# One-core transformer block with expert routing: the expert weights are transposed by VectorE in 32x32 blocks and SBUF transfers in place of TensorE, and the engines' orders are rewritten

## Chip, core, metric

The kernel runs on one core of a Trainium2 chip. The metric is the device time of one execution in microseconds (us), taken as the median over several executions. Everything is computed in fp32.

## What is computed

The input is 8 sequences of 2048 tokens with 256 features. Cut to what matters, the reference is:

```python
x = x + layernorm(attention(layernorm(x)))        # causal linear attention in chunks of 128 tokens, plus a memory part
x = x + layernorm(ffn(layernorm(x)))

def ffn(h):                                       # 4 heads, 64 keys a side, 1024 experts, 8 taken per head
    sx, ix = top_k(h @ Wq[x] @ keys[x], 8); sy, iy = top_k(h @ Wq[y] @ keys[y], 8)
    scores, indices = top_k(sx[:, None] + sy[None, :], 8)
    w = silu((h . down_embed[indices]) * softmax(scores))
    return silu(h @ W_up.T) @ W_down.T + sum(w * up_embed[indices])
```

## The kernel before

The tokens are cut into 128 tiles of 128 tokens, each tile one chunk of one sequence, sequences in turn. Nothing is gathered: for each tile and head a full row of 1024 expert weights per token is built (`wexp[:, h, :]`, 128 x 1024), which is zero outside the chosen experts. The four rows are added into `wexp[:, 3, :]`, that sum is transposed to `gT` (experts on partitions), and `y` gets the product of `gT` with the centred `up_embed` (`ue`).

The work of a tile is spread over `STAGES` = 8 steps. The helper `pipeline(body)` calls `body` once a step on each engine, with `t[k]` the tile that is in stage k at this step (the tile that entered k steps ago). Each engine has its own `body`, and the statements in it are that engine's order in a step, written out by hand. Waits on named semaphores tie the engines together.

- TensorE (PE): its products go through `product` (L511), its transposes of normed activations through `turn` (L516). In a step it multiplies with `route`, `wvo`, `wdownT`, `deT`, `state`, `mem_x`, `ue`, `wupT`, `wqT` and `wkT`. For tile `t[5]` it transposes `wexp[:, 3, :]` in eight 128x128 pieces into two PSUM banks (L587, L591), after a wait on `heads_summed`.
- ScalarE (ACT): moves PSUM to SBUF and computes Exp, Silu and Square. It copies the two transposed banks to `gT` (L692, L703). A step loads four activation tables (Silu and Exp alternate).
- VectorE (DVE): selection by threshold (`picked`) and multiplication with the softmax (`prob`), four each of 128x1024 a step (L768, L784, L843, L851; L776, L780, L788, L861), maxima, layernorm statistics.
- GpSimd (POOL): `key_sums` (L401, four of 128x1024 a step), the powers for layernorm (L387), small tensors, and it issues two accumulating transfers inside SBUF: L441 adds heads 0 and 2 to 1 and 3 (1024 KB, `head_pairs_summed`), L409 adds head 1 to 3 (512 KB, `heads_summed`).
- SyncE (SP) issues the store of `x_out` (L355) and the load of `x_in` (L360), one each a step.

The `gT` product for tile `t[6]` waits for both copies of a step before:

```python
pe.wait_ge(s_expert_weights_T_0_ready, t[6] + 1)
pe.wait_ge(s_expert_weights_T_1_ready, t[6] + 1)
product(y_ps, EC, lambda c: gT[:, t[6] % 2, c, :], lambda c: ue[:, c, :], start=False)
```

Of the kernel before, what the change touches and what calls it, by code (L numbers as in the profile page):

```python
# [6 lines left out]
def sandwich_kernel(nc, hidden, w_q, w_k, w_v, w_o, gate, memory, memory_norm,  # L7
# [33 lines left out]
    HALF = 512  # L41
    LAST_IN = EXPERTS - 1
# [8 lines left out]
    SLOTS = 4  # L51
# [11 lines left out]
    with ctx:  # L63
# [26 lines left out]
        x_mid = sb("x_mid", [P, SLOTS, D])  # L90
# [34 lines left out]
        z_last = sb("z_last", [P, NC])  # L125
        w_last = sb("w_last", [P, 2])
# [6 lines left out]
        gT = sb("gT", [P, 2, EC, P])  # L133
# [33 lines left out]
        g_ps = (bank[5], bank[3])  # L167
# [29 lines left out]
        s_mem_in_psum = sem("mem_in_psum")  # L197
        s_num_in_psum = sem("num_in_psum")
# [42 lines left out]
        s_expert_weights_T_0_in_psum = sem("expert_weights_T_0_in_psum")  # L241
        s_expert_weights_T_1_in_psum = sem("expert_weights_T_1_in_psum")
        s_expert_weights_T_0_ready = sem("expert_weights_T_0_ready")
        s_expert_weights_T_1_ready = sem("expert_weights_T_1_ready")
# [4 lines left out]
        s_x_stored = sem("x_stored")  # L249
        s_head_0_sums_ready = sem("head_0_sums_ready")  # L250
# [27 lines left out]

        def alone(eng):

            eng.sem_inc(s_passed, 1)

        STAGES = 8

        def pipeline(body):


            for step in range(TILES + STAGES - 1):
                body([t if 0 <= t < TILES else None for t in range(step, step - STAGES, -1)],
                     STAGES + SLOTS <= step < TILES)  # L290

# [3 lines left out]
        def chunk_of(t):  # L295
            return t // BATCH

        KEPT = TILES - BATCH
# [39 lines left out]
        def _(sp):  # L338
# [13 lines left out]
            def body(t, steady):  # L352
                if t[7] is not None:
                    sp.wait_ge(s_x_out_ready, t[7] + 1)
                    sp.dma_start(out_tiles[:, chunk_of(t[7]), seq_of(t[7]), :], x_out[:, :]).then_inc(s_x_stored, 16)  # L355
                if t[0] is not None:
                    wait(sp, s_x_loaded, 16 * t[0])
                    if not steady:
                        wait(sp, s_x_mid_ready, t[0] - 3)
                    sp.dma_start(x_in[:, t[0] % SLOTS, :], x_tiles[:, chunk_of(t[0]), seq_of(t[0]), :]).then_inc(s_x_loaded, 16)  # L360

# [4 lines left out]
        def _(pool):  # L366
# [39 lines left out]
            def body(t, steady):  # L406
                if t[6] is not None:
                    pool.wait_ge(s_head_pairs_summed, 16 * (t[6] + 1))
                    pool.dma_start(wexp[:, HEADS - 1, :], wexp[:, 1, :], accum_op=ALU.add).then_inc(s_heads_summed, 16)  # L409
                if t[5] is not None:  # L410
                    pool.wait_ge(s_cand_exp_ready, t[5] + 1)
                    pool.wait_ge(s_cand_mask_ready, t[5] + 1)
                    nc.gpsimd.tensor_tensor(cprob[:, :, :], cmask[:, :, :], cdif[:, :, 0:NCAND], ALU.mult).then_inc(s_cand_prob_ready, 1)  # L413
                if t[4] is not None:
                    pool.wait_ge(s_x_mid_var_eps, t[4] + 1)
                    power(LN_M, t[4] % 2).then_inc(s_x_mid_rstd, 1)
                if t[5] is not None:
                    pool.wait_ge(s_softmax_inverses, t[5] + 1)
                    pool.wait_ge(s_cand_prob_ready, t[5] + 1)
                    nc.gpsimd.tensor_tensor(z_last[:, :].rearrange("p (h n) -> p h n", h=HEADS), cprob[:, :, :],  # L420
                                            per_head(rz[:, t[5] % 2, :], NCAND), ALU.mult).then_inc(s_last_expert_in_ready, 1)
                    pool.wait_ge(s_head_0_weights_ready, t[5] + 1)
                    pool.wait_ge(s_last_expert_weight, t[5] + 1)
                    nc.gpsimd.tensor_tensor(wexp[:, 0, LAST_IN:], wexp[:, 0, LAST_IN:], w_last[:, t[5] % 2:t[5] % 2 + 1], ALU.add).then_inc(s_last_expert_added, 1)  # L424
                if t[7] is not None:
                    pool.wait_ge(s_y_var_eps, t[7] + 1)
                    power(LN_Y, t[7] % 2).then_inc(s_y_rstd, 1)
# [8 lines left out]
                if t[5] is not None:  # L436
                    pool.wait_ge(s_head_1_weights_ready, t[5] + 1)
                    pool.wait_ge(s_head_2_weights_ready, t[5] + 1)
                    pool.wait_ge(s_head_3_weights_ready, t[5] + 1)
                    pool.wait_ge(s_last_expert_added, t[5] + 1)  # L440
                    pool.dma_start(wexp[:, 1::2, :], wexp[:, 0::2, :], accum_op=ALU.add).then_inc(s_head_pairs_summed, 16)  # L441
                if t[4] is not None:
# [4 lines left out]
                    nc.gpsimd.tensor_tensor(neg_max[:, t[4] % 2, :], zero[:, :], best[:, :, 0], ALU.subtract).then_inc(s_neg_max_ready, 1)  # L447
                    key_sums(2).then_inc(s_head_2_sums_ready, 1)
                    key_sums(3).then_inc(s_head_3_sums_ready, 1)
                if t[1] is not None:  # L450
                    pool.wait_ge(s_x_var_eps, t[1] + 1)
                    power(LN_X, t[1] % 2).then_inc(s_x_rstd, 1)
                if t[3] is not None:
                    pool.wait_ge(s_mix_var_eps, t[3] + 1)
                    power(LN_O, t[3] % 2).then_inc(s_mix_rstd, 1)
# [4 lines left out]
        def _(pe):  # L460
# [60 lines left out]
            def body(t, steady):  # L521
# [367 lines left out]
```

## Time and profile before

| | |
|---|---|
| three runs | 3052.66, 3050.07, 3050.55 us; median 3050.55 us |
| profiled execution | 3049.49 us, with a span of 3047.8 us |
| busy, of the span | TensorE 98%, its weight loads 80%, ScalarE 86%, VectorE 71%, GpSimd 60% |
| mean granted TensorE clock | 0.995 of full speed |
| transfers | 244.17 MB, mean 80 GB/s |

The time of an execution is the span plus what lies around it, here 1.7 us. An engine is busy while one of its instructions runs; for TensorE matmuls overlap in the records, so a matmul's own duration is longer than the distance to the next one. The profile names an operation by its line in the kernel, its output and its inputs. An fp32 matmul stands in the trace as two records, a transpose by TensorE as one. A duration is followed in square brackets by the idle time ahead of it and by the work that ended this idle time.

### The profile page before, as it was taken

The numbers are of one execution on the slowest core, as the hardware profiler recorded it, in microseconds if no ns is written. First come the engines' busy times: TensorE is split into PE (matmuls) and PEld (weight loads), VectorE is DVE, ScalarE is ACT, GpSimd is POOL, SyncE is SP. The second block draws the span as 40 slices with busy tenths as digits, with TensorE's granted clock in tenths as the row PEclk, the third lists the DMA queues.
The fourth block names the chain that finished last, engine by engine and source line by source line (L and its number), as shares of the span: only waits on it lengthen the run. The fifth ranks groups of instructions, "written<-read, shape, count | busy, mean of one in ns | idle before, by whom it ended". The sixth has DMA issues, their size and how long they took to land.

```text
span 3047.8 us, 48454 instructions
## 1 busy us (share of the span) xinstructions
PE 3001.7 (98%) x16426; PEld 2446.1 (80%) x16426; DVE 2169.6 (71%) x5636; ACT 2622.7 (86%) x4106; POOL 1821.7 (60%) x2455
## 2 busy tenths in 40 slices
PE   6999999999999999999999999999999999999997
PEld 5788888888888888888888888888888888888886
DVE  4777777767776777777677767776777777677774
ACT  4988888888888888888888888888888888888985
POOL 2665665566566656655665666566556655665664
PEclk8999999999999999999999999999999999999999
DMA  3443444344334434443444344334434443443443
GB/s 92 81 85 73 81 83 80 77 82 83 75 77 86 81 74 79 85 80 75 81 83 78 77 84 83 74 77 87 81 73 80 83 80 77 81 83 76 82 85 71
DMA packets 96202, 244.17 MB, mean 80 GB/s; under 512 B 8659, under 2 KB 46548, under 8 KB 95956
## 3 DMA queue, kind: packets, MB, share of 16 engines
q0 software_dynamic: 53248, 201.34, 36.7%
q1 hardware_dynamic: 42708, 39.73, 4.4%
q8 instruction: 132, 2.16, 0.3%
q14 instruction: 114, 0.93, 0.1%
HBM read 22.94 MB, written 16.78 MB: 13 GB/s over the span
## 4 chain that ended last, share of the span: by engine, by line
PE 96%; DMA 1%; issue 1%; ACT 0%; POOL 0%; DVE 0%; SPq 0%; POOLq 0%; DVEq 0%
PE banks L511 84%; PE banks L563 3%; PE banks L516 2%; PE banks L547 2%; PE banks L587 2%; PE banks L591 2%; PE banks L550 1%; DMA wexp<-wexp 1%; DMA sums<-in_L_ffn_keys_dram 0%; SPq L345 0%; POOL sums L401 0%; PE banks L502 0%; PE banks L495 0%; PE banks L480 0%; DVE prob L861 0%
## 5 line engine op out<-in xcount | busy, mean ns | idle before, releaser
L401 POOL TENSOR_TENSOR sums<-scores 128x1024 f32<-128x1024 f32 x512 | 1076.6, 2218 | 392.8 <-ACT scores L636 392.8
L511 PEld LDWEIGHTS banks<-xn2T,wupT 128*128 128x128 f32 x4096 | 477.3, 192 | 9.2 <-DVE state L848 2.7
L511 PE MATMUL banks<-deT,xn2T 128*128 128x512 f32 x1024 | 481.3, 592 | 0.0
L511 PE MATMUL banks<-xn2T,wupT 128*128 128x128 f32 x4096 | 478.2, 275 | 1.9 <-DVE state L848 1.9
L511 PE MATMUL banks<-wdownT,hT 128*128 128x256 f32 x2048 | 464.4, 380 | 0.0
L511 PE MATMUL banks<-ue,gT 128*128 128x256 f32 x2048 | 462.9, 379 | 0.0
L511 PEld LDWEIGHTS banks<-wdownT,hT 128*128 128x128 f32 x2048 | 390.1, 191 | 53.7 <-issue 0.5
L511 PEld LDWEIGHTS banks<-ue,gT 128*128 128x128 f32 x2048 | 388.6, 190 | 53.8 <-issue 0.7
L387 POOL TENSOR_TENSOR rstd<-var_eps,minus_half 128x1 f32<-128x1 f32 x512 | 329.9, 704 | 56.3 <-DVE var_eps L829 38.2
L413 POOL TENSOR_TENSOR cprob<-cmask,cdif 128x112 f32<-128x112 f32 x128 | 65.9, 515 | 396.6 <-DVE cmask L751 396.6
L511 PEld LDWEIGHTS banks<-deT,xn2T 128*128 128x128 f32 x1024 | 185.3, 190 | 129.9 <-issue 122.9
L424 POOL TENSOR_TENSOR wexp<-wexp,w_last 128x1 f32<-128x1 f32 x128 | 26.2, 205 | 364.7 <-ACT z_last L696 364.7
L511 PE MATMUL banks<-route,xn2T 128*128 128x512 f32 x512 | 242.2, 596 | 0.7 <-ACT xn2T L700 0.7
L804 DVE SCALAR_TENSOR_TENSOR sig<-banks,rqk 128x512 f32<-128x512 f32 x128 | 88.5, 691 | 193.9 <-ACT banks L642 193.9
L843 DVE SCALAR_TENSOR_TENSOR picked<-sums,cand_best,banks 128x1024 f32<-128x1024 f32 x128 | 163.9, 1280 | 62.0 <-PE banks L511 62.0
L654 ACT COPY sk_nat<-banks 128x256 f32<-128x256 f32 x120 | 44.6, 372 | 176.1 <-PE banks L550 176.1
L820 DVE TENSOR_SCALAR dens<-banks 128x2 f32<-128x2 f32 x128 | 20.5, 160 | 246.6 <-PE banks L547 246.6
L788 DVE SCALAR_TENSOR_TENSOR prob<-picked,rz,prob 128x1024 f32<-128x1024 f32 x128 | 164.5, 1285 | 13.7 <-DVE picked L784 0.5
L682 ACT ACT_TABLE_LOAD x128 | 164.2, 1283 | 2.3
L650 ACT ACT_TABLE_LOAD x127 | 162.9, 1283 | 2.2
L861 DVE SCALAR_TENSOR_TENSOR prob<-picked,rz,prob 128x1024 f32<-128x1024 f32 x128 | 164.3, 1284 | 0.0
L776 DVE SCALAR_TENSOR_TENSOR prob<-picked,rz,prob 128x1024 f32<-128x1024 f32 x128 | 163.9, 1281 | 0.0
(140 smaller groups left out, 7244.3 us busy)
## 6 DMA issues: line engine op xcount, KB each, us to landing
wexp<-wexp POOLq DMA_DIRECT2D x128, 1024.0 KB, 7.9
wexp<-wexp POOLq DMA_DIRECT2D x128, 512.0 KB, 4.7
x_in<-_attn_hidden_states_dram SPq DMA_DIRECT2D x128, 128.0 KB, 2.1
out_dram<-x_out SPq DMA_DIRECT2D x128, 128.0 KB, 1.7
wexp<-in_L_ffn_W_up_dram SPq DMA_DIRECT2D x1, 1024.0 KB, 7.1
prob<-in_L_ffn_down_embed_dram SPq DMA_DIRECT2D x1, 1024.0 KB, 9.6
ue<-in_L_ffn_up_embed_dram SPq DMA_DIRECT2D x1, 1024.0 KB, 12.0
wexp<-in_L_ffn_W_down_dram SPq DMA_DIRECT2D x1, 1024.0 KB, 13.0
```

Source lines behind the costliest of these rows:

```text
L387: return nc.gpsimd.tensor_tensor(rstd[:, n, m:m + 1], var_eps[:, n, m:m + 1], minus_half[:, :], ALU.pow)
L401: return nc.gpsimd.tensor_tensor(sums[:, k, :, :], scores[:, k, 0:XIN].unsqueeze(2).broadcast_to([P, XIN, NKEYS]), scores[:, HEADS + k, :] ...
L413: nc.gpsimd.tensor_tensor(cprob[:, :, :], cmask[:, :, :], cdif[:, :, 0:NCAND], ALU.mult).then_inc(s_cand_prob_ready, 1)
L511: last = nc.tensor.matmul(out, lhs(c), rhs(c), start=(start and c == 0), stop=(stop and c == chunks - 1))
L563: last = nc.tensor.matmul(ds_ps[:, c, :], sk_nat[:, c * P:(c + 1) * P], v_one[:, :], start=True, stop=True)
L650: nc.scalar.activation(cdif[:, :, :], cdif[:, :, :], ACT.Exp).then_inc(s_cand_exp_ready, 1)
L682: nc.scalar.activation(flat(hT[:, t[4] % 2, 4:8, :]), u_ps[1][:, :], ACT.Silu).then_inc(s_hidden_1_ready, 1)
L776: nc.vector.scalar_tensor_tensor(prob[:, 1, :], picked[:, 1, :], rz[:, t[5] % 2, 1:2], prob[:, 1, :], ALU.mult, ALU.mult).then_inc(s_head_ ...
L788: nc.vector.scalar_tensor_tensor(prob[:, 3, :], picked[:, 1, :], rz[:, t[5] % 2, 3:4], prob[:, 3, :], ALU.mult, ALU.mult).then_inc(s_head_ ...
L804: nc.vector.scalar_tensor_tensor(sig[:, t[3] % 2, :, :], eqk, 1.0, rqk[:, :, :], ALU.min, ALU.add).then_inc(s_sigma_ready, 1)
L843: nc.vector.scalar_tensor_tensor(picked[:, 0, :], head(sums, 0), best[:, 0, TOP - 1:TOP], down, ALU.is_ge, ALU.mult).then_inc(s_head_0_sel ...
L861: nc.vector.scalar_tensor_tensor(prob[:, 0, :], picked[:, 0, :], rz[:, t[4] % 2, 0:1], prob[:, 0, :], ALU.mult, ALU.mult).then_inc(s_head_ ...
```

## The change

- The eight PE transposes and the two ACT copies are gone, and with them four semaphores. DVE now transposes all 32x32 blocks of `wexp[:, 3, :]` in one instruction into a new SBUF tensor `w_blocks`; it waits for `heads_summed` and for the moves of the tile before.
- SP then moves the blocks between groups of 32 partitions: sixteen transfers a step, each of 32 rows of 1 KB.
- `gT` is laid out `[P, 2, P, EC]` (token, then chunk), so that a row of a moved block is contiguous. The stationary operand of the `ue` product is `gT[:, s, :, c]`, whose 128 elements in a partition are 8 elements (32 bytes) apart.
- The pipeline has 10 stages in place of 8, `x_in` has 8 slots in place of 4, and `x_mid` has 8.
- The order of all engines in a step is rewritten, and several operations belong to another stage than before.

```diff
-    SLOTS = 4
+    SLOTS = 8
+    MID_SLOTS = 8
...
+        w_blocks = sb("w_blocks", [P, EXPERTS])
...
-        gT = sb("gT", [P, 2, EC, P])
+        gT = sb("gT", [P, 2, P, EC])
...
+        def moved(eng, sems, t, dmas, most=TILES):
+
+            if 0 <= t < most:
+                eng.wait_ge(sems[t % 2], 16 * dmas * (t // 2 + 1))
...
-        STAGES = 8
+        STAGES = 10
...
+                if t[7] is not None:
+                    sp.wait_ge(s_expert_weights_blocks_turned, t[7] + 1)
+                    for i in range(BLOCKS):
+                        for j in range(BLOCKS):
+                            sp.dma_start(gT[j * BLOCK:(j + 1) * BLOCK, t[7] % 2, i * BLOCK:(i + 1) * BLOCK, :],
+                                         w_blocks[i * BLOCK:(i + 1) * BLOCK, j * BLOCK * EC:(j + 1) * BLOCK * EC]
+                                         .rearrange("p (t c) -> p t c", c=EC)).then_inc(s_expert_weights_blocks_moved[t[7] % 2], 16)
...
-                if t[5] is not None:
-                    pe.wait_ge(s_heads_summed, 16 * (t[5] + 1))
-                    for k in range(4):
-                        e = k
-                        last = nc.tensor.transpose(g_ps[0][:, k * P:(k + 1) * P], wexp[:, HEADS - 1, e * P:(e + 1) * P], ident[:, :])
-                    last.then_inc(s_expert_weights_T_0_in_psum, 1)
...
+                if t[3] is not None:
+                    pe.wait_ge(s_xn1T_ready, t[3] + 1)
+                    product(v_ps, DC, lambda c: xn1T[:, c, :], lambda c: wvo[:, c, :]).then_inc(s_v_in_psum, 1)
+                    wait(pe, s_hidden_1_ready, t[3] - 1)
...
+                if t[7] is not None:
+                    moved(pe, s_expert_weights_blocks_moved, t[7], BLOCKS ** 2)
+                    product(y_ps, EC, lambda c: gT[:, t[7] % 2, :, c], lambda c: ue[:, c, :], start=False).then_inc(s_y_in_psum, 1)
...
+                    wait(act, s_expert_weights_blocks_turned, t[6])
+                    nc.scalar.activation(wexp[:, 3, :], prob[:, 3, :], ACT.Silu).then_inc(s_head_3_weights_ready, 1)
...
-                    act.wait_ge(s_expert_weights_T_0_in_psum, t[5] + 1)
-                    nc.scalar.copy(flat(gT[:, t[5] % 2, 0:4, :]), g_ps[0][:, :]).then_inc(s_expert_weights_T_0_ready, 1)
...
+            def blocks(x):
+                return x.rearrange("p (c j q) -> p j c q", j=BLOCKS, q=BLOCK)
+
+            def turned_blocks(x, chunks):
+                return x[:, :].rearrange("p (j t c) -> p j c t", j=BLOCKS, c=chunks)
+
...
+                    dve.wait_ge(s_heads_summed, 16 * (t[7] + 1))
+                    moved(dve, s_expert_weights_blocks_moved, t[7] - 1, BLOCKS ** 2)
+                    nc.vector.transpose(turned_blocks(w_blocks, EC), blocks(wexp[:, HEADS - 1, :])).then_inc(s_expert_weights_blocks_turned, 1)
```

TensorE before, from the product with `ue` to the next step's first products (`wupT` gives the hidden layer, `ident` marks a transpose):

```order
L511 MATMUL banks<-ue,gT 128x256 [waits expert_weights_T_1_ready,expert_weights_T_0_ready]
L511 MATMUL banks<-ue,gT 128x256 x7
L511 MATMUL banks<-xn2T,wupT 128x128 [waits state_ready]
L511 MATMUL banks<-xn2T,wupT 128x128 x15
L587 MATMUL banks<-ident,wexp 128x128 [waits heads_summed]
L587 MATMUL banks<-ident,wexp 128x128 x3
L591 MATMUL banks<-ident,wexp 128x128 x4
L516 MATMUL banks<-ident,xn 128x128 [waits xn2_ready,xn1T_ready]
L516 MATMUL banks<-ident,xn 128x128
L511 MATMUL banks<-xn1T,wqT 128x128 [waits hidden_1_ready,xn1T_ready]
```

And in the changed kernel, from the first half of the `wupT` products to the transpose of `xn2`, behind which `state` and `route` follow:

```order
L523 MATMUL banks<-xn2T,wupT 128x128 [waits state_ready]
L523 MATMUL banks<-xn2T,wupT 128x128 x7
L523 MATMUL banks<-wvo,xn1T 128x256 [waits xn1T_ready]
L523 MATMUL banks<-wvo,xn1T 128x256
L523 MATMUL banks<-xn1T,wqT 128x128 [waits hidden_1_ready]
L523 MATMUL banks<-xn1T,wqT 128x128 x3
L523 MATMUL banks<-xn1T,wkT 128x128 x4
L523 MATMUL banks<-xn2T,wupT 128x128 x8
L523 MATMUL banks<-ue,gT 128x256 [waits expert_weights_blocks_moved_1]
L523 MATMUL banks<-ue,gT 128x256 x7
L528 MATMUL banks<-ident,xn 128x128 [waits xn2_ready]
```

The transposes are gone, the `wupT` products stand in two halves with `wvo` and the `wqT`, `wkT` products between them, and the wait on `hidden_1_ready` (the Silu of the first half, which frees its PSUM bank) stands two `wvo` matmuls behind that half.

GpSimd in the changed kernel, from the candidate differences of a tile (behind its first two key sums) to the power that the next `xn2` waits for (`cmask` of DVE is waited for as cand_mask_ready):

```order
L466 TENSOR_TENSOR cdif<-cand_best 128x144 [waits best_ready]
L421 TENSOR_TENSOR wexp<-wexp,w_last 128x1 [waits head_0_weights_ready,last_expert_weight]
L423 TENSOR_TENSOR neg_max<-zero,cand_best 128x4
L429 DMA wexp<-wexp 128x2x1024 [waits head_1_weights_ready,head_3_weights_ready,head_2_weights_ready,last_expert_added]
L412 TENSOR_TENSOR sums<-scores 128x1024
L398 TENSOR_TENSOR rstd<-var_eps,minus_half 128x1 [waits mix_var_eps]
L438 TENSOR_TENSOR cprob<-cmask,cdif 128x112 [waits cand_mask_ready,cand_exp_ready]
L412 TENSOR_TENSOR sums<-scores 128x1024
L442 TENSOR_TENSOR z_last<-cprob,rz 128x112 [waits softmax_inverses,cand_prob_ready]
L446 DMA wexp<-wexp 128x1024 [waits head_pairs_summed]
L398 TENSOR_TENSOR rstd<-var_eps,minus_half 128x1 [waits x_var_eps]
L398 TENSOR_TENSOR rstd<-var_eps,minus_half 128x1 [waits x_mid_var_eps]
```

The power for `xn2` (waits x_mid_var_eps) now stands behind the issue of the second accumulating transfer, which waits for the first to land.

SyncE in the changed kernel, a step and the start of the next:

```order
L361 DMA x_in<-in_L_attn_hidden_states_dram 128x256 [waits x_loaded]
L364 DMA out_dram<-x_out 128x256 [waits x_out_ready]
L369 DMA gT<-w_blocks 32x256 [waits expert_weights_blocks_turned]
L369 DMA gT<-w_blocks 32x256 x15
L361 DMA x_in<-in_L_attn_hidden_states_dram 128x256 [waits x_loaded]
```

The sixteen moves are new on this queue; the load of `x_in` stands ahead of the store.

## Rows read from the trace of the kernel before

**Rows 1.** First part of the page: busy time of each engine.

```profile
PE 3001.7 (98%) x16426; PEld 2446.1 (80%) x16426; DVE 2169.6 (71%) x5636; ACT 2622.7 (86%) x4106; POOL 1821.7 (60%) x2455
```

**Rows 2.** Busy time by stretch: PE, PEld, DVE, ACT, POOL, granted clock, DMA share, GB/s.

```profile
190.00:1400.00 1210.00, 1210.00 (x6649) 987.11 (x6648) 876.81 (x2280) 1062.24 (x1664) 735.95 (x988) 1.00 0.42 80
```

**Rows 3.** Waits of TensorE for others: us in total, times, longest us.

```profile
PE banks L587 <- DMA wexp<-wexp: 13.4, 3, 10.5
```

**Rows 4.** Chain that ended last, one step: start us, us, what.

```profile
1535.82 11.73 PE banks L511 x56
...
1558.04 0.44 PE banks L587 x4
1558.47 0.44 PE banks L591 x4
...
1559.13 11.73 PE banks L511 x56
```

**Rows 5.** Timeline of TensorE, same step: start us, us, engine, line, operation.

```profile
1539.16 1.03 PE L511 MATMUL banks<-wvo,xn1T 128*128 128x256 f32 x4
1540.03 3.62 PE L511 MATMUL banks<-wdownT,hT 128*128 128x256 f32 x16
...
1550.85 3.62 PE L511 MATMUL banks<-ue,gT 128*128 128x256 f32 x16
1554.30 3.73 PE L511 MATMUL banks<-xn2T,wupT 128*128 128x128 f32 x32
```

**Rows 6.** Groups by line: busy us, mean ns of one, idle before.

```profile
L682 ACT ACTIVATE hT<-banks 128x512 f32<-128x512 f32 x128 | 76.4, 597 | 1.4
L703 ACT COPY gT<-banks 128x512 f32<-128x512 f32 x128 | 76.1, 595 | 0.3 <-PE banks L591 0.3
L387 POOL TENSOR_TENSOR rstd<-var_eps,minus_half 128x1 f32<-128x1 f32 x512 | 329.9, 704 | 56.3 <-DVE var_eps L829 38.2 <-ACT y_sq L688 14.4 <-DVE var_eps L763 2.1
L861 DVE SCALAR_TENSOR_TENSOR prob<-picked,rz,prob 128x1024 f32<-128x1024 f32 x128 | 164.3, 1284 | 0.0
L729 DVE SCALAR_TENSOR_TENSOR ue<-row_sum,ue 128x2048 f32<-128x2048 f32 x1 | 2.3, 2291 | 0.0
```

**Rows 7.** Timeline near the end: ScalarE hands over to the waiting TensorE.

```profile
2995.71 0.36 ACT L700 COPY xn2T<-banks 128x256 f32<-128x256 f32 x1
2996.12 0.30 PEld L511 LDWEIGHTS banks<-route,xn2T 128*128 128x128 f32 x2 [0.90 <-ACT xn2T L700]
```

**Rows 8.** Timeline of the SP queue, at the start and in the step of rows 4.

```profile
1.95 0.47 SPq L345 DMA_DIRECT2D sums<-in_L_attn_memory_dram  x1
2.45 0.46 SPq L345 DMA_DIRECT2D sums<-in_L_attn_w_q_dram  x1
...
1539.63 0.43 SPq L360 DMA_DIRECT2D x_in<-_attn_hidden_states_dram  x1
```

**Rows 9.** DMA issues: KB each, median us from issue to landing.

```profile
wexp<-wexp POOLq DMA_DIRECT2D x128, 1024.0 KB, 7.9
wexp<-wexp POOLq DMA_DIRECT2D x128, 512.0 KB, 4.7
x_in<-_attn_hidden_states_dram SPq DMA_DIRECT2D x128, 128.0 KB, 2.1
...
sums<-in_L_attn_w_q_dram SPq DMA_DIRECT2D x1, 256.0 KB, 3.7
```

**Rows 10.** Timeline of GpSimd in the same step.

```profile
1540.02 1.90 POOL L401 TENSOR_TENSOR sums<-scores 128x1024 f32<-128x1024 f32 x1 [3.03 <-ACT scores L636]
1541.88 1.02 POOL L434 TENSOR_TENSOR cand_best<-top 128x64 f32<-128x64 f32 x4
```

**Rows 11.** Timeline of TensorE at the very end.

```profile
3033.17 1.12 PE L587 MATMUL banks<-ident,wexp 128*128 128x128 f32 x4 [10.47 <-DMA wexp<-wexp]
...
3034.94 5.07 PE L511 MATMUL banks<-wdownT,hT 128*128 128x256 f32 x16
3039.85 3.62 PE L511 MATMUL banks<-ue,gT 128*128 128x256 f32 x16
```

More of the change, by code:

```diff
@@ L521, in body @@
             def body(t, steady):
+                if t[5] is not None:
+                    product(d_ps[0], DC, lambda c: xn2T[:, t[5] % 2, c, :], lambda c: deT[:, c, 0:HALF]).then_inc(s_down_0_in_psum, 1)
+                if t[4] is not None:
+                    wait(pe, s_sk_ready, t[4] + 1, KEPT)
+                    pe.wait_ge(s_mix_memory_part, t[4] + 1)
+                    if t[4] < KEPT:
+                        for c in range(DC):
+                            last = nc.tensor.matmul(ds_ps[:, c, :], sk_nat[:, c * P:(c + 1) * P], v_one[:, :], start=True, stop=True)
+                        last.then_inc(s_state_add_in_psum, 1)
@@ new lines, in body @@
+                if t[5] is not None:
+                    wait(pe, s_state_ready, t[5] + 2, KEPT)
+                    for k in range(4):
+                        ic = 4 + k
+                        last = product(u_ps[1][:, k * P:(k + 1) * P], DC, lambda c: wupT[:, c, ic * P:(ic + 1) * P],
+                                       lambda c: xn2T[:, t[5] % 2, c, :])
+                    last.then_inc(s_up_1_in_psum, 1)
+                if t[3] is not None:
+                    pe.wait_ge(s_xn1T_ready, t[3] + 1)
+                    product(v_ps, DC, lambda c: xn1T[:, c, :], lambda c: wvo[:, c, :]).then_inc(s_v_in_psum, 1)
+                    wait(pe, s_hidden_1_ready, t[3] - 1)
+                    if not steady:
+                        wait(pe, s_state_ready, t[3], KEPT)
+                    for side, w in enumerate((wqT, wkT)):
+                        for ec in range(DC):
+                            col = (side * DC + ec) * P
+                            last = product(qk_ps[:, col:col + P], DC, lambda c: w[:, c, ec * P:(ec + 1) * P], lambda c: xn1T[:, c, :])
+                    last.then_inc(s_qk_in_psum, 1)
@@ new lines, in body @@
+                if t[5] is not None:
+                    for k in range(4):
+                        ic = k
+                        last = product(u_ps[0][:, k * P:(k + 1) * P], DC, lambda c: wupT[:, c, ic * P:(ic + 1) * P],
+                                       lambda c: xn2T[:, t[5] % 2, c, :])
+                    last.then_inc(s_up_0_in_psum, 1)
+                if t[7] is not None:
+                    moved(pe, s_expert_weights_blocks_moved, t[7], BLOCKS ** 2)
+                    product(y_ps, EC, lambda c: gT[:, t[7] % 2, :, c], lambda c: ue[:, c, :], start=False).then_inc(s_y_in_psum, 1)
@@ L593, in body @@
[L593 to L604 removed]
+                    product(d_ps[1], DC, lambda c: xn2T[:, t[4] % 2, c, :], lambda c: deT[:, c, HALF:]).then_inc(s_down_1_in_psum, 1)
@@ L701, in body @@
[L701 to L706 removed]
+                    act.wait_ge(s_head_2_sums_ready, t[5] + 1)
```

486 lines of the change are left out of this document (215 added, 271 removed).

## Prediction

> **What bounds the kernel now.** The page's first part comes first: TensorE is busy 98% of the span, ScalarE 86%, VectorE 71%, GpSimd 60% [rows 1]. A busy share is an average, so the stretch from 190 to 1400 us is read next: there TensorE is busy in all of the 1210 us, at the full granted clock (1.00, the 2.4 GHz level) [rows 2]. The waits say the same from the other side: TensorE's longest wait in total on the expert weights is 13.4 us, in three pieces, one of them 10.5 us at the very end [rows 3, 11]. The chain that ended last runs through TensorE alone in a step, from 1535.82 to the same place at 1559.13 [rows 4]. So one step is 23.31 us, and TensorE's own work fills it. What shortens that work shortens the step, until another engine or a loop of waits needs as long. By rows 2, ScalarE works 1062.24/1210 of a step, 20.5 us, and VectorE 876.81/1210, 16.9 us.
>
> **The change, part by part.**
>
> The eight transposes are two pieces of the chain, 0.44 and 0.44 us [rows 4]. They sit on the path: 0.88 us a step, 128 tiles, **112.6 us less**. The new step of TensorE alone is 23.31 - 0.88 = 22.43 us.
>
> The two copies of ScalarE (595 ns each [rows 6], less where they overlap a neighbour) take its 20.5 us to some 19.4. It is hidden under TensorE before and after, so it is worth nothing by itself. It is what lets ScalarE follow a shorter step: 3 us stay free in it.
>
> VectorE's new instruction has no row. From below it is bounded by a 128x1024 operation, 1.28 us; from above I take twice a stream of 2048 elements, 4.6 us, since every output lands 32 bytes from the last and nothing here writes so [rows 6]. I take 1.3, because the element count is that of the nearer row. VectorE then has 18.2 us of work, 21.5 at the upper end. It stands ahead of the maxima over the scores, and these have to wait for the `route` product anyway. At 1.3 us it costs nothing; if that cover goes, each us beyond some 2.5 delays the maxima, the candidates and in the end the mask that TensorE waits for.
>
> The sixteen moves: one issue on SP takes 0.43 us, and issues in a row start 0.50 us apart [rows 8], so 16 take 8 us. A load of 128 KB lands in 2.1 us [rows 9]; I take that for the last of 32 KB. The moved blocks are there 10.1 us after the transpose ends. The chain by hand, from the start of a TensorE step: the transpose ends at some 18, the moves at 28.5, and the product with `ue` starts in the next step at 22.4 + 12.4 = 34.8. Some 6 us of slack: hidden. Were they slower by more than that, TensorE would stand at `ue`. What is queued on SP behind them is the next load, with eight slots in place of four, and the next store, which starts nearly a step later: no cost. The moves' bounds are nothing and, one after the other at 2.1 us each, 33.6 us.
>
> The Trainium skill speaks against these transfers: "DMA: Bandwidth & Descriptors", section Rules for kernel authors, says that transfers under 64 KB mostly pay overhead and should be joined. Were that overhead paid one by one, the sum would be the fourth rival's. The trace disagrees at this place: two loads start 0.50 us apart, and one of them takes 3.7 us to land [rows 8, 9], so their latencies overlap.
>
> The new place of a wait is where I do charge something. The `wqT` products wait for the Silu that empties the bank of the first `wupT` half, and only the two `wvo` matmuls stand between. A half is (1554.30 to the end of 32 records at 3.57 us)/2 = 1.79 us, its last record ends 0.16 later, and `wvo` covers 0.87 [rows 5]. The Silu takes 0.60 [rows 6], and ScalarE to TensorE costs 0.05 and a weight load of some 0.1 to the first matmul [rows 7]. So TensorE could go on 2.66 us after the half began, and may go on after 1.79 + 0.16 + 0.05 + 0.60 + 0.05 + 0.1 = 2.75. Bounds: nothing, and 1.3 us if ScalarE comes late by one table load. I take 0.1, since ScalarE has 0.8 us to spare there by my walk: **12.8 us more**. All that TensorE has queued behind waits too; that is the whole step.
>
> The other waits of TensorE, walked through a step in the same way with the durations above: `xn2T` 0.15 us to spare, the mask 0.8, `mix` 0.6, `state` 1.8, `xn2` some 2. The next one late would be `xn2`. Its power stands on GpSimd behind the second accumulating transfer. Scores ready at 19.4, then key sums, candidates, key sums (1.86, 0.96, 1.86 [rows 10]) and small ones: the first transfer is issued at 24.8. It lands 7.9 later [rows 9]; the second issue, two powers of 0.70 [rows 6] and the normalisation are at most 3 us more: 35.7 to 36.4, needed at 38.3.
>
> The ends. Before, the last sum is there at 3033.17, then come `wdownT` and `ue`, to 3043.5 [rows 11]. Now 1.3 + 8 + 2.1 go by first, with `wdownT` beside them, and then 3.6 for `ue`: 3048.2. **5 us more.** Stages are not steps: from `route` to `ue` of one tile it was 60 us and is 3 x 22.5 - 4.5 = 63. **3 us more**; the fill is otherwise the same chain. Bounds 0 and 20.
>
> The sum on the profiled execution's own time: 3049.49 - 112.6 + 12.8 + 5 + 3 = 2957.7 us. The median of the runs shown lies 1.1 above it: **2959 us**.
>
> **The rivals.**
>
> *A loop of waits takes part of it back.* The moves' 512 KB run into the first accumulating transfer. The second one, of that size, takes 4.7 us [rows 9]; with half of this added, the power for `xn2` is late by 0.3 to 0.5 us. At 0.5 a step: 2959 + 64 = 3023. For it: two hand-overs of my walk have under 0.2 us of slack, and the order is new everywhere. Against: 3 us free in ScalarE, 4 in VectorE, and the moves mostly end before that transfer starts. If all 4.7 were added, a step would be over 24 us and the kernel slower; that is a small part of the last case below.
>
> *The weight loads of `gT` become slow: the other side.* TensorE now loads the stationary `gT` with 32 bytes between elements; before, every load read contiguous elements. The 128-column products carry a load per record at 3.57/32 = 0.11 us, and `ue` gives each load 3.45/16 = 0.216 us [rows 5]. So a load may take twice as long unseen. It decides from where sixteen loads eat the 0.73 us left of the gain: 0.216 + 0.046 = 0.26 us each, 2.4 times today's. At three times, 0.33, it is 16 x 0.118 = 1.9 us a step: 2959 + 243 = 3200 us. Against: the loads leave half of the time free. No row here reads a strided operand, for or against.
>
> "Advanced Engine Details and Errata" of the Trainium skill, section SBUF Cachelines, is on this rival's side: at least two hits on a 16-byte line are needed to hide the access, and here each element is on a line of its own. It gives no factor, and no row here shows one.
>
> *It does not do what it says.* TensorE waits for the blocks as long as it transposed: SP would need 6 us more than I gave it and 0.8 on top. 3050 us. Against: 8 us of issues in a step of 22.
>
> *The moves pay their latency one by one.* 33.6 us a step would be SP's, 128 x 33.6 = 4300 us. Against: rows 8 and 9 as above.
>
> **How the numbers follow.** Forecast 0.62; loop of waits, still faster, 0.20; no change 0.03; slow weight loads 0.10; moves one by one 0.02; the accumulating transfer fully delayed or a transpose near 4.6 us, slower, 0.03. Faster 0.82, same 0.03, slower 0.15, with 0.2% (6 us) as what a measurement here can tell from no change. The range reaches from 3049.49 - 112.6 + 1.1 = 2938 (no added wait, no longer end) over the forecast and the loop of waits to 3045, a step of 23.1 us; together 0.82.
>
> **What would show it.** The chain repeats every 22.5 us and stays on TensorE; 112 us of transposes and both `gT` copies are gone; TensorE shows a short wait for ScalarE's Silu at `wqT` and none for the moves. The 128x1024 transpose takes 1.3 us. SP's sixteen issues take 8 us and end 6 us ahead of `ue`. Records of the `ue` product still start 0.216 us apart; more would be the slow loads. A wait of TensorE for `xn2` in every step is the loop. I am wrong on the mechanism if the step is above 22.8 us, and wrong on the side if `ue` takes over 4.3 us in place of 3.45.

## The result and the profile after

The changed kernel takes 3066.59 us (median of 4 runs, 3066.05 to 3070.97), the kernel before 3050.31 beside it (3050.04 to 3052.66): a ratio of 1.0054 with a 95% interval of 1.0039 to 1.0069. It is slower by 0.5%, where 2959 us was forecast. Its profiled execution spans 3064.6 us at a mean granted clock of 0.992.

The first part of the page, which answers to [rows 1], and the same stretch as in [rows 2] (TensorE, weight loads, VectorE, ScalarE and GpSimd busy, granted clock, DMA share, GB/s):

```profile
PE 2980.1 (97%) x15402; PEld 2433.9 (79%) x15402; DVE 2430.1 (79%) x5764; ACT 2534.2 (83%) x3854; POOL 1957.3 (64%) x2455
```

```profile
190.00:1400.00 1210.00, 1203.01 (x6250) 985.50 (x6250) 983.02 (x2343) 1026.57 (x1564) 794.08 (x988) 1.00 0.51 103
```

1024 TensorE instructions are gone, some 112 us of them by the forecast, and yet TensorE is busy for only 21.6 us less than in [rows 1]: its other work has grown. The granted clock is 1.00 in that stretch as before, so the clock is no part of it. TensorE is no longer busy all the time either: 7 of 1210 us are missing. DMA is up from 80 to 103 GB/s.

The groups by line show where it is. `L777` is the new transpose, `L825` has its pair in `L861` of [rows 6]:

```profile
L523 PE MATMUL banks<-ue,gT 128*128 128x256 f32 x2048 | 536.4, 415 | 43.9 <-DMA gT<-w_blocks 43.3
L523 PEld LDWEIGHTS banks<-ue,gT 128*128 128x128 f32 x2048 | 503.8, 336 | 55.8 <-DMA gT<-w_blocks 52.3
...
L777 DVE STREAM_TRANSPOSE w_blocks<-wexp 128x1024 f32<-128x1024 f32 x128 | 260.9, 2038 | 7.1 <-DMA gT<-w_blocks 3.6 <-DMA wexp<-wexp 3.4
L825 DVE SCALAR_TENSOR_TENSOR prob<-picked,rz,prob 128x1024 f32<-128x1024 f32 x128 | 192.1, 1500 | 0.0
```

In the kernel before, the same two rows of the `ue` product were:

```profile
L511 PE MATMUL banks<-ue,gT 128*128 128x256 f32 x2048 | 462.9, 379 | 0.0
L511 PEld LDWEIGHTS banks<-ue,gT 128*128 128x128 f32 x2048 | 388.6, 190 | 53.8 <-issue 0.7 <-ACT mix L656 0.2
```

Two things are seen at once. A load of `gT` takes 336 ns in place of 190, and the product itself 536.4 us in place of 462.9: that is 73.5 us more for the same 2048 records. And 43.3 us of idle time stand before it, ended by the moves, where there was none; 20.7 of them are three waits at the very end, shown below. Of the waits (total, times, longest), these are new or have grown:

```profile
POOL wexp L446 <- DMA wexp<-wexp: 60.5, 104, 7.7
...
PE banks L523 <- DMA gT<-w_blocks: 43.3, 32, 14.6
...
PEld banks L523 <- ACT hT L689: 28.9, 126, 0.6
```

TensorE waits for the moves 32 times, not once a step. Most steps do without, as this one on TensorE's timeline, which answers to [rows 5]:

```profile
1552.39 1.03 PE L523 MATMUL banks<-wvo,xn1T 128*128 128x256 f32 x4
1553.25 1.14 PE L523 MATMUL banks<-xn1T,wqT 128*128 128x128 f32 x8
1554.23 1.06 PE L523 MATMUL banks<-xn1T,wkT 128*128 128x128 f32 x8
...
1556.91 4.11 PE L523 MATMUL banks<-ue,gT 128*128 128x256 f32 x16
1560.86 0.38 PE L528 MATMUL banks<-ident,xn 128*128 128x128 f32 x2
```

From `wqT` to `wkT` it is 0.98 us, where eight records of 0.11 are 0.88: the 0.1 for the wait on `hidden_1_ready`, as forecast. `ue` holds TensorE from 1556.91 to 1560.86, 3.95 us; in [rows 5] it was 1550.85 to 1554.30, 3.45. The step is 23.01 us (from one `route` product at 1538.94 to the next at 1561.95) in place of 23.31. So a good step gains 0.30 us of the 0.78 forecast.

SP's queue in the same step, to be held against [rows 8]; the first row is the store, the last the next load:

```profile
1536.34 0.35 SPq L364 DMA_DIRECT2D out_dram<-x_out  x1
1540.69 14.24 SPq L369 DMA_DIRECT2D gT<-w_blocks  x16
1554.98 0.65 SPq L361 DMA_DIRECT2D x_in<-_attn_hidden_states_dram  x1
```

The sixteen issues take 14.2 us, not 8, and end 2 us ahead of `ue`, not 6. The last block of this step lands at 1556.63, 0.3 us before `ue` starts: nothing is left. The DMA issues (KB each, median us to landing), against [rows 9]:

```profile
wexp<-wexp POOLq DMA_DIRECT2D x128, 1024.0 KB, 8.9
gT<-w_blocks SPq DMA_DIRECT2D x2048, 32.0 KB, 1.9
```

The first accumulating transfer has gone from 7.9 to 8.9 us. The 1.9 us are the median of all moves, and not what counts: of the sixteen of a step, the last lands 4.5 us after its issue in the median, and from the first issue to the last landing it is 16.0 us, where 10.1 were forecast. The trace has the reason beside it. In the step above the first accumulating transfer is issued in the midst of the moves:

```profile
1547.10 1.24 POOL L429 DMA_DIRECT2D wexp<-wexp  x1
```

Of the 678 moves that were issued while that transfer was under way, 399 took SP over 1 us, and they landed after 5.2 us in the median. Of the other 1370, 30 took over 1 us, and they landed after 1.8. Both are slower where they meet, and the run with four moves below bears this out; in the median step eight of the sixteen moves are in flight beside the transfer.

Where the transfer takes still longer, the slack is less than nothing. The chain that ended last, in such a stretch (start, us, what):

```profile
349.82 4.21 PE banks L523 x16
...
363.12 10.15 DMA wexp<-wexp
...
373.56 0.90 POOL wexp L446
374.45 1.63 POOL rstd L398 x3
...
379.05 1.96 DVE w_blocks L777
381.02 0.51 SPq L369
...
392.15 5.97 DMA gT<-w_blocks
398.12 0.04 issue
398.17 2.05 PE banks L523 x7
```

This is a closed loop over two steps. `ue` is late at 349.82; the `route` product, the key sums and the candidates behind it are late; the first accumulating transfer is issued at 363.12 and takes 10.15 us. GpSimd waits for it, and only then issues the second transfer and raises the three powers. VectorE waits for one of the powers, and has the transpose behind it. Then come the issues, the last of them 11.1 us after the first, with a landing of 5.97, and the next `ue` but one is late at 398.17. The loop needs 48.35 us for two steps, 24.2 each, which is more than TensorE's own 23.0.

The very end, against [rows 11], is slower as well. (The 6.74 us of the second `ue` are in part the clock: from 3040 to 3050 the granted clock is 0.60, so mostly the 1.2 GHz level, after 14.62 us in which TensorE stood idle.)

```profile
3017.73 5.41 PE L523 MATMUL banks<-ue,gT 128*128 128x256 f32 x16 [2.96 <-DMA gT<-w_blocks]
...
3042.01 6.74 PE L523 MATMUL banks<-ue,gT 128*128 128x256 f32 x16 [14.62 <-DMA gT<-w_blocks]
...
3056.07 4.21 PE L523 MATMUL banks<-ue,gT 128*128 128x256 f32 x16 [3.08 <-DMA gT<-w_blocks]
```

To see where the time lies, I cut every span at the first record of each `route` product: the stretch to the first one, ten steps, 111 steps in the middle, the last six, and the rest. In us:

```
                  first   10 steps   111 steps (median)   last 6    rest    span
before            53.3     225.5     2585.2   (23.31)     132.1     51.7   3047.8
after             56.9     228.3     2575.7   (23.01)     141.5     62.3   3064.6
e5_both_off       58.0     224.0     2498.8   (22.53)     128.2     53.7   2962.7
e6_pairs_later    61.1     227.1     2499.0   (22.53)     128.2     64.0   2979.5
```

The 111 steps gain only 9.5 us, with a mean of 23.20 against a median of 23.01 and single steps up to 24.45; everything around them loses 26. (The two lower kernels are experiments, below.) The first column is no measure of the change: with the old order and another read of `gT` in `ue` alone, as in two runs below, the first `route` product came at 58.0 and 57.6 us, where it came at 53.3 here, so 4.7 us lie between executions of the same work.

### The profile page after: what moved, and what is told of

Read it like the earlier page. It is cut to its first block, busy times and chain, and to the rows that moved or that the text cites. A ratio compares the mean times of both kernels' runs of the same rounds, so it can differ in the third digit from the quotient of the medians.

```text
span 3064.6 us, 48288 instructions
## 1 busy us (share of the span) xinstructions
PE 2980.1 (97%) x15402; PEld 2433.9 (79%) x15402; DVE 2430.1 (79%) x5764; ACT 2534.2 (83%) x3854; POOL 1957.3 (64%) x2455
## 4 chain that ended last, share of the span: by engine, by line
PE 69%; DMA 10%; SPq 8%; POOL 5%; DVE 4%; issue 3%; ACT 1%; DVEq 0%; POOLq 0%
PE banks L523 63%; SPq L369 8%; DMA wexp<-wexp 6%; DMA gT<-w_blocks 4%; PE banks L541 2%; POOL sums L412 2%; DVE w_blocks L777 1%; PE banks L528 1%; PE banks L602 1%; POOL rstd L398 1%; DVE prob L772 1%; DVE prob L768 1%; PE banks L595 1%; POOL wexp L446 1%; POOL cand_best L462 1%
## 5 line engine op out<-in xcount | busy, mean ns | idle before, releaser
L523 PE MATMUL banks<-ue,gT 128*128 128x256 f32 x2048 | 536.4, 415 | 43.9 <-DMA gT<-w_blocks 43.3
L523 PEld LDWEIGHTS banks<-ue,gT 128*128 128x128 f32 x2048 | 503.8, 336 | 55.8 <-DMA gT<-w_blocks 52.3
L398 POOL TENSOR_TENSOR rstd<-var_eps,minus_half 128x1 f32<-128x1 f32 x512 | 492.3, 1108 | 67.2 <-DVE var_eps L849 32.1
L523 PEld LDWEIGHTS banks<-xn2T,wupT 128*128 128x128 f32 x4096 | 487.4, 192 | 10.1 <-DVE state L815 3.6
L777 DVE STREAM_TRANSPOSE w_blocks<-wexp 128x1024 f32<-128x1024 f32 x128 | 260.9, 2038 | 7.1 <-DMA gT<-w_blocks 3.6
L805 DVE SCALAR_TENSOR_TENSOR picked<-sums,cand_best,banks 128x1024 f32<-128x1024 f32 x128 | 163.9, 1280 | 85.2 <-PE banks L523 85.1
L689 ACT ACTIVATE hT<-banks 128x512 f32<-128x512 f32 x128 | 76.4, 597 | 147.9 <-PE banks L523 147.8
L752 DVE SCALAR_TENSOR_TENSOR picked<-sums,cand_best,banks 128x1024 f32<-128x1024 f32 x128 | 163.9, 1280 | 35.7 <-POOL sums L412 35.7
L825 DVE SCALAR_TENSOR_TENSOR prob<-picked,rz,prob 128x1024 f32<-128x1024 f32 x128 | 192.1, 1500 | 0.0
L633 ACT COPY xn2T<-banks 128x256 f32<-128x256 f32 x128 | 47.7, 373 | 166.7 <-PE banks L528 166.7
L429 POOL DMA_DIRECT2D wexp<-wexp x128 | 158.4, 1237 | 27.8 <-issue 7.4
L781 DVE MAX8 top<-scores 128x8 f32<-128x16 f32 x512 | 83.7, 163 | 104.8 <-ACT scores L647 104.6
```

The lines of the kernel that those rows point to most:

```text
L398: return nc.gpsimd.tensor_tensor(rstd[:, n, m:m + 1], var_eps[:, n, m:m + 1], minus_half[:, :], ALU.pow)
L523: last = nc.tensor.matmul(out, lhs(c), rhs(c), start=(start and c == 0), stop=(stop and c == chunks - 1))
L689: nc.scalar.activation(flat(hT[:, t[5] % 2, 4:8, :]), u_ps[1][:, :], ACT.Silu).then_inc(s_hidden_1_ready, 1)
L752: nc.vector.scalar_tensor_tensor(picked[:, 0, :], head(sums, 2), best[:, 2, TOP - 1:TOP], down, ALU.is_ge, ALU.mult).then_inc(s_head_2_sel ...
L777: nc.vector.transpose(turned_blocks(w_blocks, EC), blocks(wexp[:, HEADS - 1, :])).then_inc(s_expert_weights_blocks_turned, 1)
L781: nc.vector.max(top[:, 0, k, :], scores[:, k, 0:XIN])
```

## The experiments

Two suspects stand in the trace, the strided loads and the moves. The first four runs take each away or give it to the other kernel. Times of before beside the two groups of four runs were 3051.76 and 3052.36 us.

**Loads contiguous, all else as after** (each load then takes the wrong expert weights, as many as before).

```
- product(y_ps, EC, lambda c: gT[:, t[7] % 2, :, c], ...
+ product(y_ps, EC, lambda c: gT[:, t[7] % 2, c * (P // EC):(c + 1) * (P // EC), :].rearrange("p t c -> p (t c)"), ...
```

> The changed kernel, with one edit: the stationary operand of the ue product is read as 128 contiguous elements of gT in place of 128 elements 32 bytes apart. It computes with wrongly ordered expert weights; everything else is as in the changed kernel (3066.6 us). Theory A (slow strided weight loads cost what the forecast left out): the sixteen records of that product start 0.216 us apart again in place of 0.247, a step loses 0.5 us, and the time falls by 128 x 0.5 = 64 us to about 3003. Theory B (the chain transpose, sixteen issues, landing sets the step, and the loads only lie beside it): the product gets shorter but TensorE waits as much longer for the moved blocks; 3045 us or more.

Measured: 3020.59 us, 0.9901 [0.9886, 0.9916] of before, which is 46 us less than after.

```profile
L523 PEld LDWEIGHTS banks<-ue,gT 128*128 128x128 f32 x2048 | 386.3, 194 | 116.0 <-DMA gT<-w_blocks 66.4
...
PE banks L523 <- DMA gT<-w_blocks: 55.8, 46, 14.4
```

The load is back at 194 ns, and the median step at 22.54. But the wait for the moves has grown from 43.3 to 55.8 us: a faster TensorE stands at `ue` more often, so part of the gain is given back.

**Loads strided by 32 bytes in the kernel before**, which has no moves:

```
- product(y_ps, EC, lambda c: gT[:, t[6] % 2, c, :], ...
+ product(y_ps, EC, lambda c: gT[:, t[6] % 2, :, :].rearrange("p c t -> p (c t)").rearrange("p (t c) -> p t c", c=EC)[:, :, c], ...
```

> The kernel before, with one edit: the stationary operand of the ue product is read with 32 bytes between its elements (wrongly ordered expert weights, all else as before; no moves in SBUF). Theory A: TensorE fills the step, so 16 loads a step that are 0.03 us too long each add 0.5 us a step: 3050.5 + 64 = 3115 us. Theory B: strided loads hide under the matmuls; 3050 us, within 0.2%.

Measured: 3099.06 us, 1.0153 [1.0136, 1.017], 47 us more than the kernel before.

```profile
L511 PEld LDWEIGHTS banks<-ue,gT 128*128 128x128 f32 x2048 | 500.8, 336 | 4.0 <-ACT mix L656 0.2 <-issue 0.2
```

```profile
1508.74 4.00 PE L511 MATMUL banks<-ue,gT 128*128 128x256 f32 x16
```

The same 336 ns, and `ue` at 4.00 us for 3.62. The step goes from 23.31 to 23.69, +0.38, with no other wait in it. So the price belongs to the read itself. It was expected at 0.5 a step from the changed kernel's row and came out smaller.

**Four moves of 128 rows in place of sixteen of 32**, loads strided as after (the same bytes; each block goes from its own rows to its own rows):

```
- for j in range(BLOCKS):
-     sp.dma_start(gT[j * BLOCK:(j + 1) * BLOCK, t[7] % 2, i * BLOCK:(i + 1) * BLOCK, :], w_blocks[i * BLOCK:(i + 1) * BLOCK, j * BLOCK * EC:(j + 1) * BLOCK * EC] ...
+ sp.dma_start(gT[:, t[7] % 2, i * BLOCK:(i + 1) * BLOCK, :], w_blocks[:, i * BLOCK * EC:(i + 1) * BLOCK * EC] ...
```

> The changed kernel with four moves of 128 rows in place of sixteen of 32 rows: the same bytes and the same number of 1 KB rows, but no block changes its partitions, so the expert weights are wrong. Theory B (SP's sixteen issues, 12 to 14 us a step, make the blocks late): the issues take about 3 us, TensorE's waits for the moved blocks (43 us) go, and the time falls to 3010 to 3025 us. Theory A: what is too much lies in the loads; 3060 us or more. Third theory (the moved bytes slow the accumulating transfers and with them the loop): issues are short, but the first accumulating transfer still lands after 8.9 us, and the time stays above 3050.

Measured: 3025.58 us, 0.9913 [0.9898, 0.9928], 41 us less than after.

```profile
wexp<-wexp POOLq DMA_DIRECT2D x128, 1024.0 KB, 8.0
...
gT<-w_blocks SPq DMA_DIRECT2D x512, 128.0 KB, 2.1
```

```profile
PE banks L522 <- DMA gT<-w_blocks: 2.6, 1, 2.6
```

```profile
1532.15 2.40 SPq L368 DMA_DIRECT2D gT<-w_blocks  x4
```

```profile
1538.82 1.24 POOL L428 DMA_DIRECT2D wexp<-wexp  x1
```

One wait is left, no middle step is longer than 23.01, and the first accumulating transfer lands in 8.0 us. This run does not say whether 512 KB beside that transfer would slow it: the four moves, issued in 2.4 us and landed 2.1 after their issue, are over before it starts, in 127 of the 128 steps. What it shows is that moves which do not meet the transfer neither delay it nor are delayed. The blocks also stay in their own partitions here, so number, time and way of the moves changed together.

**`gT` in pairs, a layout for the real computation.** Two chunks stand side by side, so that a load reads every 8 bytes; the transpose is two instructions of 128x512, each of them writing 8 bytes apart:

```
- gT = sb("gT", [P, 2, P, EC])
+ gT = sb("gT", [P, 2, EC // 2, P, 2])
...
- product(y_ps, EC, lambda c: gT[:, t[7] % 2, :, c], ...
+ product(y_ps, EC, lambda c: gT[:, t[7] % 2, c // 2, :, c % 2], ...
```

> The changed kernel with gT and w_blocks laid out in pairs of chunks: the loads read every second element (8 bytes apart), VectorE writes every second element in two instructions, and a moved row of 1 KB lands in four pieces of 256 bytes. The result is the reference's. Theory A: loads of 8-byte stride cost what contiguous ones cost (two elements of a 16-byte line are hit), 64 us less as in the first run, if the moves keep up. Theory B: four times as many pieces make the moves slower, issues take 14 us or more a step, TensorE's waits for moved blocks grow, and the time is 3066 us or above.

Measured: 3015.02 us (3007.98 to 3018.36), 0.9877 [0.9862, 0.9891].

```profile
L523 PEld LDWEIGHTS banks<-ue,gT 128*128 128x128 f32 x2048 | 395.0, 198 | 92.3 <-DMA gT<-w_blocks 54.7
...
L778 DVE STREAM_TRANSPOSE w_blocks<-wexp 128x512 f32<-128x512 f32 x256 | 167.1, 694 | 11.2 <-DMA wexp<-wexp 7.6 <-DMA gT<-w_blocks 3.5
```

At 8 bytes a load costs next to nothing more (198 ns, `ue` back at 3.62), and the transpose of the same 1024 elements takes 2 x 0.694 = 1.39 us for 2.04. TensorE still waits 44.5 us for the moves.

**Both taken away**: the edits of the first and the third run together.

> The changed kernel with both edits of the first and third run: contiguous loads of gT and four moves of 128 rows (expert weights wrong, bytes and work as in the changed kernel). If the two costs are separate and all there is, the time is 3066.6 - 46 - 41 = 2980 us. If the moves also ate part of what contiguous loads give (TensorE waited for blocks instead), the steps in the middle are 22.54 us without spread, and first route at 57, ten steps in 224.5, 111 x 22.54, six steps in 129, tail 52 give 2966 us. A third cost that neither run took away would leave steps above 22.6 us.

Measured: 2965.68 us, 0.9715 [0.9701, 0.973], 101 us less than after. The median of the middle steps is 22.53, and none is longer than 22.55. With this the four kernels make a square:

```
                   sixteen moves   four moves
strided loads         3066.59        3025.58
contiguous loads      3020.59        2965.68
```

The loads cost 60 us where nothing else holds TensorE (right column, 0.47 a step) and 46 where the moves do; the moves cost 55 us beside contiguous loads and 41 beside strided ones. The two cover each other by 14 us. (The runs stem from three groups, in which the kernel before took 3050.3 to 3052.4 us.)

**The pairs kernel one stage later: throughput or latency?** The last run leaves out where a block goes, so it can't tell whether the moves are too many or only too late. This one keeps the pairs and all sixteen moves, and lets `wdownT`, `ue` and all behind them run one stage later (`hT` gets four slots, and SP waits for the `ue` of the tile before the last, which read the same one of the two slots of `gT`):

```
- STAGES = 10
+ STAGES = 11
...
- moved(pe, s_expert_weights_blocks_moved, t[7], BLOCKS ** 2)
+ moved(pe, s_expert_weights_blocks_moved, t[8], BLOCKS ** 2)
```

> The kernel with pairs of chunks (3015.0 us, result as the reference's), and the products with wdownT and ue one stage later, with four slots of hT: the blocks have a whole step more to land, the transfers are the same. If what spreads the steps is TensorE's wait for the moved blocks, that wait goes and the middle steps are 22.54 us: 111 x 0.22 = 25 us less, about 2990. If it is the accumulating transfers that the moves delay (8.9 in place of 7.9 us), the waits come back elsewhere (normalised xn2, scores), and the time stays near 3015.

Measured: 2975.24 us (2973.54 to 2981.26), 0.9745 [0.9729, 0.9762]. It leaves nothing of the computation out and beats both kernels, the one before by 2.5%. (Its profiled execution is the longest of the four, 2981.26 us.)

```profile
wexp<-wexp POOLq DMA_DIRECT2D x128, 1024.0 KB, 8.8
```

```profile
PE banks L524 <- DMA gT<-w_blocks: 3.1, 1, 3.1
```

```profile
1528.86 13.16 SPq L370 DMA_DIRECT2D gT<-w_blocks  x16
```

The issues take as long as before and the accumulating transfer still lands in 8.8 us, and neither costs anything: the step is 22.53. What was short was the time from the transpose to `ue`. Against the profile of the pairs kernel, the middle steps give back 27.8 us and the last six 11.4; the new stage itself costs 5 (0.5 to the first `route` product, 2.8 in the first ten steps, 1.5 after the last).

**Four of the sixteen moves from ScalarE's queue**, on the pairs kernel, ahead of the Silu of head 3:

```
+ for k in range(BLOCKS ** 2 - 4, BLOCKS ** 2):
+     i, j = k // BLOCKS, k % BLOCKS
+     nc.scalar.dma_start(gT[j * BLOCK:(j + 1) * BLOCK, t[7] % 2, :, i * BLOCK:(i + 1) * BLOCK, :], ...
```

> The kernel with pairs of chunks (3015.0 us, result as the reference's), with four of the sixteen moves issued by ScalarE ahead of its Silu of head 3. If the length of SP's row of issues is the cost, the last block is there some 3 us earlier, waits for moved blocks (44.5 us) fall below 15 and the time is 2990 to 3000 us. If ScalarE's time is what is short, its four issues (2 us or more a step) make head 3, the first accumulating transfer and the loop later: 3015 us or more.

Measured: 3106.1 us, 1.017 [1.0155, 1.0185], 91 us more than with SP alone. A miss.

```profile
PE banks L543 <- ACT mix L679: 97.6, 118, 1.3
...
PE banks L525 <- DMA gT<-w_blocks: 17.0, 5, 9.3
```

```profile
1548.19 1.40 ACTq L668 DMA_DIRECT2D gT<-w_blocks  x2
...
1549.63 1.28 ACTq L668 DMA_DIRECT2D gT<-w_blocks  x2
1550.95 1.06 ACT L672 ACTIVATE wexp<-prob 128x1024 f32<-128x1024 f32 x1 [1.60 <-issue]
```

The wait for the moves did fall, from 44.5 to 17.0 us. But four issues hold ScalarE's instructions back for 2.7 us, its Silu stands idle for 1.60 of that, `mix` behind it is late, and TensorE now waits for `mix` in nearly every step (23.57 us). ScalarE was busy 84% of the pairs kernel's span; the share did not say that this place in its order has nothing to give.

**Every 16 bytes, in the kernel before.** Where between 8 and 32 bytes does the load become slow?

```
+ product(y_ps, EC, lambda c: gT[:, t[6] % 2, :, :].rearrange("p c t -> p (c t)").rearrange("p (d t c) -> p d t c", d=2, c=4)[:, c // 4, :, c % 4], ...
```

> The kernel before, with one edit: the stationary operand of the ue product is read with 16 bytes between its elements (wrongly ordered expert weights). The run with 32 bytes took 3099 us and 336 ns a load. If a load slows as soon as no two elements share 16 bytes, this one does the same, 336 ns and 3099 us; if it slows by distance, it lies between 192 and 336 ns; if 16 bytes are still free, 3051 us.

Measured: 3086.69 us, 1.0114 [1.0098, 1.0129]; the step is 23.58, +0.27.

```profile
L511 PEld LDWEIGHTS banks<-ue,gT 128*128 128x128 f32 x2048 | 487.6, 327 | 4.0 <-ACT mix L656 0.2 <-issue 0.2
```

A load of 128x128 takes 190 ns contiguous, 198 at 8 bytes, 327 at 16 and 336 at 32. The step lies between 8 and 16 bytes, where two neighbours stop sharing 16 bytes. "Advanced Engine Details and Errata" of the Trainium skill, section SBUF Cachelines, says that at least two hits on a 16-byte line are needed to absorb the access latency; these four numbers agree.

## Why the prediction was wrong, point by point

**The range and the side were wrong; the steady step without the two suspects was right.** It was forecast at 22.5 us and is 22.53 with both taken away, where the whole kernel takes 2965.68 us for the 2959 forecast. From there the forecast misses 60 us for the loads and 55 for the moves, less the 14 by which they cover each other: 2965.7 + 60 + 55 - 14 = 3066.7.

**The step that failed first: "a load may take twice as long unseen".** I set 0.216 us per matmul against 0.11 per load and let the load cost nothing until it was 2.4 times as long. The load's own record went up by only 336/190 = 1.8 and is seen all the same: `ue` took 0.38 us more in the kernel before, 0.47 to 0.50 in the changed one. Sixteen loads are 16 x 0.146 = 2.3 us longer, so some five sixths stay hidden and a sixth to a fifth does not. A threshold at twice the time was wrong: at 327 and 336 ns, 1.7 and 1.8 times, there is a price already (0.27 and 0.38 us a step). The rival that named the strided read had the mechanism right and its threshold and size wrong: it asked for 0.26 us a load and gave 0.10 of the chances. The mark I had set for this, "over 4.3 us in place of 3.45", was not reached (3.95), and the kernel was slower still: since I had priced it alone, it had to eat the whole gain. What hides the rest of a load I can't say, nor why the changed kernel pays 0.1 us a step more than the one before for the same 336 ns.

**The second: "some 6 us of slack" at the moves.** Three of its terms were too small. The transpose took 2.04 us, not 1.3, at a place between my two bounds; the pairs point to the output stride (1.39 us at 8 bytes), though there the work is also cut into two instructions. An issue of a move took 0.59 us, not the 0.43 or 0.50 of a load, and single ones up to 2.1: 10 to 15 us in all (median 12.7), not 8. And the last of the sixteen landed after 4.5 us (median) in place of 2.1. I took the issue rate from [rows 8], where no other large transfer was beside it. From the start of the transpose to the last block it is 2.04 + 16.0 = 18.0 us in the median, where I had 1.3 + 8 + 2.1 = 11.4: that is the 6 us. Behind two of the three terms stands one sentence, "the moves mostly end before that transfer starts". It was mistaken by its own clock, which had the moves from 18 to 28.5 and the transfer at 24.8; in the trace half of the moves are in flight beside it.

**The loop of waits came, by another way round.** I had it as the second accumulating transfer that delays the power for `xn2`. In the chain it is the first one that grows (8.9 us, and 10.15 in the stretch shown), and GpSimd, standing at its landing, raises its powers late; VectorE waits for one of them ahead of the transpose. So it goes over the moves back to `ue`. The rival's size was 64 us; the moves cost 41 to 55. My sum had charged the moves to no one, because I walked one step with single durations; the loop runs over two steps. In the stretch shown one transfer of 10 us is in it; that this transfer alone tips the kernel over was not isolated.

**"112.6 us less" was counted over 128 steps.** It holds for the middle: 111 x 0.78 = 86.6 forecast, 2585.2 - 2498.8 = 86.4 measured with both suspects away. The first ten and last six steps gain 5.4, not 16 x 0.78 = 12.5; that is about the 7 us between 2959 and 2965.7. I had read the steady stretch alone. In the kernel before, TensorE was busy throughout in most of these steps too; they were shorter (22.44 and 22.22 us) since the products with `state` are absent for the first eight tiles, and others for the last. In the new order those `state` products stand between the transpose of `xn2` and `route`, and cover ScalarE's copy to `xn2T` between the two. Where they are absent, TensorE waits for that copy, and a step stays at 22.44 although the eight transposes are gone (from the trace with both suspects away):

```profile
145.94 0.38 PE L527 MATMUL banks<-ident,xn 128*128 128x128 f32 x2
146.88 1.96 PE L522 MATMUL banks<-route,xn2T 128*128 128x512 f32 x4 [0.55 <-ACT xn2T L632]
```

"`xn2T` 0.15 us to spare" was walked through a step that has the `state` products.

**Three slips in the sums change nothing.** Moves that start at 18 and take 10.1 us are there at 28.1, not 28.5; the gain that slow loads had to eat was 0.72 us a step with the ends and 0.78 without, not 0.73; and 3045 us is a step of 23.2, not 23.1. The mean of the middle steps was just that, 23.20: what put the kernel past the range lies outside the middle steps.

**What held.** The wait for the Silu at `wqT`: 28.9 us in 126 waits, 0.23 a step, stand before the weight loads, and 0.10 of it is left in the step, 22.53 against 22.43; I took 0.1. ScalarE and the VectorE work stayed hidden in the steady step: no wait for either is in it beyond that Silu. The ends did not hold, even where their sum looks right. Without the suspects they are longer by 4.7 us at the start, which is no more than lies between executions, and by 2.0 behind the last `route` product, together 6.7 for the 8 forecast: that is luck. With sixteen moves the stretch behind the last `route` product is 10.6 us longer, where I had 5.

**What stays open.** Moves and accumulating transfer delay each other where they overlap: with none, four and eight moves in flight (median) the transfer takes 8.0, 8.3 and 8.8 to 8.9 us (four moves, four from ScalarE, all others). Which part of the way they contend for was not isolated. And the `prob` product of head 3 on VectorE (`L825`) takes 1500 ns where it took 1284, with contiguous loads as well (1503 ns). No run was made for it, but the traces show where: in 125 of 128 steps it runs while GpSimd goes from a key sum to the power behind it, and both are long.

```profile
1547.89 2.38 POOL L412 TENSOR_TENSOR sums<-scores 128x1024 f32<-128x1024 f32 x1
1549.76 2.00 POOL L398 TENSOR_TENSOR rstd<-var_eps,minus_half 128x1 f32<-128x1 f32 x1
```

```profile
1549.97 1.39 DVE L825 SCALAR_TENSOR_TENSOR prob<-picked,rz,prob 128x1024 f32<-128x1024 f32 x1
```

In the run with four moves from ScalarE the same product comes later: 1.28 us in the 110 steps in which GpSimd stands idle beside it, 1.89 in the 12 that meet both operations. TensorE does not wait for it in either kernel's steady step.

## What to carry to other kernels

A new layout has a reader as well as a writer: look at the stride at which TensorE's stationary operand is read, and keep two elements of it within 16 bytes. A chain of many small transfers is to be costed with issues and landings beside the transfers that it meets, and around the whole loop of who waits for whom, not across one step; where only latency is short, run the consumer a stage later. Before a gain is multiplied by the number of steps, look at the first and last steps: products that are absent there may be the ones that cover a hand-over.

## What the runs showed of the hardware

- A 128x128 fp32 weight load took 190 ns contiguous, 198 at 8-byte, 327 at 16-byte and 336 at 32-byte distance, and the long ones cost 17 to 31 ns per load (0.27 to 0.50 us over sixteen) although matmuls of 0.216 us run beside them.
- VectorE's 32x32 transposes of 1024 fp32 elements a row took 2.04 us with outputs 32 bytes apart and 2 x 0.694 us with 8 bytes.
- Issuing a 32 KB move inside SBUF took SP 0.59 us (median; 0.51 to 2.11) and ScalarE 0.63 (0.59 to 0.86), where it also held ScalarE's computing instructions back (1.60 us idle before a Silu).
- Sixteen such moves, eight of them in flight beside a 1 MB accumulating transfer, took it from 7.9 to 8.9 us. Moves issued beside it landed after 5.2 us in place of 1.8, and most took SP over 1 us to issue.
- A 128x1024 operation of VectorE took 1.28 us alone and 1.49 (mean) beside the change of GpSimd from a key sum to a power; the power took 2.00 us there, and 0.61 in a step of the run with four moves from ScalarE, where the two did not meet.
